# One channel scale and one channel bias per half step on VectorE, over two tiles at once, in the layer passes of a spectral image network

## The reference, cut to what matters

```
def layer_norm(x, g, b):
    mu = jnp.mean(x, axis=-1, keepdims=True)
    var = jnp.mean((x - mu) ** 2, axis=-1, keepdims=True)
    return (x - mu) * jax.lax.rsqrt(var + EPS) * g + b
...
for i in range(LAYERS):
    w1 = w1r[i] + 1j * w1i[i]
    w2 = w2r[i] + 1j * w2i[i]
    x1 = spectral_conv(h, w1, w2)
    x2 = jnp.einsum('bchw,oc->bohw', h, conv_w[i]) + conv_b[i][None, :, None, None]
    h = x1 + x2
    h = jnp.transpose(h, (0, 2, 3, 1))
    h = layer_norm(h, ln_g[i], ln_b[i])
    if i < LAYERS - 1:
        h = gelu(h)
    h = jnp.transpose(h, (0, 3, 1, 2))
```

## Time and profile before

| | |
|---|---|
| median of 3 runs | 3648.15 us (3635.49 to 3648.17) |
| profiled execution: its time, its span | 3639.14 us, 3637.3 us |
| PE busy | 3132.9 us, 86% |
| DVE busy | 2467.3 us, 68% |
| ACT busy | 2218.8 us, 61% |
| POOL busy | 2127.3 us, 58% |

### The profile page before, as it was taken

One profiled execution on the slowest core, in us unless ns is written; L12 is line 12 of the kernel. 1 busy time (PEld: TensorE's weight loads), 2 busy tenths in 40 slices (PEclk: granted clock), 3 DMA queues, 4 the chain that ended last, 5 costly groups with the idle time before them and its releaser, 6 DMA issues. The chain is left out here.

```text
span 3637.3 us, 202203 instructions
## 1 busy us (share of the span) xinstructions
PE 3132.9 (86%) x86496; PEld 2151.1 (59%) x86496; DVE 2467.3 (68%) x3756; ACT 2218.8 (61%) x3645; POOL 2127.3 (58%) x1147
## 2 busy tenths in 40 slices
PE   6777777999968999968999958999999986999998
PEld 3555556777756777756777753333333334666666
DVE  6665547888847888847888844444444436999996
ACT  4455445777745777746777736777777773555554
POOL 2322216888847888838888834444444434555554
PEclk8888887999988999979999978999999997999998
DMA  2232234555544556545555641211121111000000
GB/s 83 94 93 93 88 128 131 169 168 168 172 149 135 169 174 171 171 137 146 168 168 172 174 133 47 60 56 52 54 58 54 54 28 41 13 12 12 12 12 9
DMA packets 206411, 366.15 MB, mean 101 GB/s; under 512 B 107186, under 2 KB 124146, under 8 KB 206018
## 3 DMA queue, kind: packets, MB, share of 16 engines
q1 hardware_dynamic: 194610, 350.25, 32.5%
q10 hardware_dynamic: 7920, 10.03, 0.9%
q0 software_dynamic: 3744, 3.84, 0.7%
HBM read 206.31 MB, written 157.71 MB: 100 GB/s over the span
## 5 line engine op out<-in xcount | busy, mean ns | idle before, releaser
L1296 POOL TENSOR_TENSOR rstd<-var,mhalf 128x16 f32<-128x16 f32 x512 | 1537.4, 3018 | 773.9 <-DVE var L1073 767.2
L571 PE MATMUL ps<-d,hp 128*32 128x48 f32 x32768 | 492.9, 211 | 89.7 <-ACT asb L812 41.7
L571 PEld LDWEIGHTS ps<-d,hp 128*32 128x32 f32 x32768 | 410.2, 112 | 207.6 <-issue 106.3
L1073 DVE TENSOR_REDUCE var<-sq 128x16 f32<-128x528 f32 x384 | 402.8, 1050 | 146.3 <-ACT sq L772 146.2
L812 ACT COPY asb<-ps 128x384 f32<-128x384 f32 x512 | 254.3, 497 | 386.9 <-PE ps L571 264.8
L1087 DVE TENSOR_TENSOR zt<-ps,rstd 128x512 f32<-128x512 f32 x512 | 351.4, 686 | 200.0 <-POOL rstd L1296 195.5
L546 PE MATMUL ps<-ident,hp 128*128 128x128 f32 x2048 | 377.9, 309 | 12.7 <-ACT ho L796 10.0
L496 PEld LDWEIGHTS ps<-cwl,hc 64*64 64x64 f32 x16384 | 273.4, 139 | 146.9 <-issue 136.3
L772 ACT ACTIVATE sq<-ps 128x512 f32<-128x512 f32 x512 | 288.0, 599 | 115.4 <-PE ps L496 81.7
L507 PEld LDWEIGHTS ps<-dyi,gt 64*48 64x48 f32 x16384 | 234.7, 125 | 202.0 <-issue 190.0
L479 PE MATMUL ps<-zb,ex 48*128 48x512 f32 x1024 | 303.5, 668 | 53.8 <-issue 34.8
(11 more groups left out here) (171 smaller groups left out, 4881.3 us busy)
## 6 DMA issues: line engine op xcount, KB each, us to landing
h_scratch<-ho SPq DMA_DIRECT2D x256, 512.0 KB
hc<-h_scratch SPq DMA_DIRECT2D x256, 512.0 KB, 4.4
wsb<-in_w SPq DMA_DIRECT2D x64, 288.0 KB
gin<-g_scratch SPq DMA_DIRECT2D x252, 72.0 KB
gin<-g_scratch SPq DMA_DIRECT2D x504, 36.0 KB
g_scratch<-hp SPq DMA_DIRECT2D x32, 192.0 KB, 3.4
g_scratch<-hp ACTq DMA_DIRECT2D x32, 192.0 KB, 4.1
tokens<-wsb SPq DMA_DIRECT2D x256, 4.0 KB
```

What stands on the lines that cost most here:

```text
L571: last = nc.tensor.matmul(a_ps[row:row + 32, 2 * TRIG * k:2 * TRIG * k + 2 * TRIG], hp[b][:, u, 8 * j + k].rearrange("p v r -> p (v r)"), ...
L1073: nc.vector.tensor_reduce(dst, src, axis=AX.X, op=ALU.add).then_inc(var_ready, 1)
L1296: nc.gpsimd.tensor_tensor(rstd[u][:], var[u][:], mhalf[:], ALU.pow).then_inc(rstd_ready, 1)
```

## The change

`gain` and `bias` are no longer called once for each tile but once for each half step, over both tiles of `zt[h]` (128 x 1024 elements, with the 32 channel values spread over tiles and pixels by strides of zero). They stand behind the second `normalise`. A gelu of either tile waits for the one `bias` of its half step. The semaphores count accordingly.

```
-                act.wait_ge(zt_ready, 4 * (rank(s, g) - PAIRS) + 2 * h + u + 1)
+                act.wait_ge(zt_ready, 2 * (rank(s, g) - PAIRS) + h + 1)
...
-            def gain(s, g, h, u):
+            def gain(s, g, h):
 
-                z = zt[h][:, u].rearrange("p (c n) -> p c n", c=C)
-                dve.wait_ge(norm_ready, 4 * rank(s, g) + 2 * h + u + 1)
-                nc.vector.tensor_tensor(z, z, channels(s, 0).unsqueeze(2).to_broadcast([128, C, 16]), ALU.mult
+                z = zt[h][:].rearrange("p u (c n) -> p u c n", c=C)
+                dve.wait_ge(norm_ready, 4 * rank(s, g) + 2 * h + 2)
+                nc.vector.tensor_tensor(z, z, channels(s, 0).unsqueeze(1).unsqueeze(3).to_broadcast([128, 2, C, 16]), ALU.mult
                                         ).then_inc(gain_ready, 1)
...
                     here, old = where(i, p, 0, 0), where(i, p, 0, 1)
                     if old:
                         normalise(s, *old, 0)
-                        gain(s, *old, 0)
-                        bias(s, *old, 0)
                     if here:
                         reduce(s, *here, 0)
                     if old:
                         normalise(s, *old, 1)
-                        gain(s, *old, 1)
-                        bias(s, *old, 1)
+                        gain(s, *old)
+                        bias(s, *old)
                     if here:
                         reduce(s, *here, 1)
...
                     if here:
                         reduce(s, *here, 1)
                     if old:
-                        gain(s, *old, 1)
+                        gain(s, *old)
                     if nxt := where(i, p, 0, -2):
                         z_copy(s, nxt[0])
                     if old:
-                        bias(s, *old, 1)
+                        bias(s, *old)
```

More of the change, by code:

```diff
@@ L1115, in channels, with bias @@
                 return gbx[:, bass.ds(s, 1), which, :].rearrange("p a c -> p (a c)")
-            def gain(s, g, h, u):
-                z = zt[h][:, u].rearrange("p (c n) -> p c n", c=C)
-                dve.wait_ge(norm_ready, 4 * rank(s, g) + 2 * h + u + 1)
-                nc.vector.tensor_tensor(z, z, channels(s, 0).unsqueeze(2).to_broadcast([128, C, 16]), ALU.mult
+            def gain(s, g, h):
+                z = zt[h][:].rearrange("p u (c n) -> p u c n", c=C)
+                dve.wait_ge(norm_ready, 4 * rank(s, g) + 2 * h + 2)
+                nc.vector.tensor_tensor(z, z, channels(s, 0).unsqueeze(1).unsqueeze(3).to_broadcast([128, 2, C, 16]), ALU.mult
                                         ).then_inc(gain_ready, 1)
[L1124 to L1128, removed]
+            def bias(s, g, h):
+                z = zt[h][:].rearrange("p u (c n) -> p u c n", c=C)
+                dve.wait_ge(gain_ready, 2 * rank(s, g) + h + 1)
+                nc.vector.tensor_tensor(z, z, channels(s, 1).unsqueeze(1).unsqueeze(3).to_broadcast([128, 2, C, 16]), ALU.add
                                         ).then_inc(zt_ready, 1)
@@ L1269, in _ @@
             nc.vector.tensor_scalar(xsb[:, 0, :], xsb[:, 0, :], stem_gb[:, 3:4], None, ALU.add).then_inc(dc_ready, 1)
-            dve.sem_inc(gain_ready, 4 * PAIRS)
+            dve.sem_inc(gain_ready, 2 * PAIRS)
             dve.wait_ge(late_in, NLATE)
```

## The result

| | before | changed |
|---|---|---|
| median | 3647.64 us (3635.49 to 3648.17, 4 runs) | 4164.46 us (4158.39 to 4169.87, 4 runs) |
| profiled execution, its span | 3639.14, 3637.3 us | 4169.87, 4168.1 us |
| mean granted clock | 0.933 | 0.861 |

The changed kernel is slower: the ratio is 1.141, with a 95% interval of 1.1384 to 1.1436. The forecast was 4095 us, in a range of 3920 to 4250 us.

The account below looks back on a forecast made before the run. The prediction took a pass to be bound by PE. It summed 3639 us before, 288 for longer pairs, 5 for the last pairs and 158 for the clock to 4090, stated as 4095 us, range 3920 to 4250.

Parts of the forecast that it names:

- The operation over 1024 elements: On DVE, one merged gain or bias was taken at 1.22 us, like a plain add of 128 x 1024.
- The chain: Even half step, square through reduction, normalise, gain, bias, gelu and hc_copy to PE's turn: 6.12 us, before 2.73, turn 3.39 later.
- What is given back: After absorbed waits on ACT and PE, a pair gets 2.94 to 3.39 us longer, taken as 3.1; 93 pairs make 288 us.
- The clock's term: PE's clock falls behind the new idle gap: 5 us lower per pair at 0.34 us each, 1.7 us, 158 us in all.
- the 5 us of the last pairs: In each pass's last pair the gelu waits for four operations, not three short ones: 1.7 us, three times.
- The bound of 10 us: Rival: clock mostly at the lower level, 10 us in a pair, costing 3.5 us each; 4259 us, chance 0.1.
- The wait of L546 for L796: Sign in the later profile: PE waits for ACT's copy about 3.4 us once a pair, near 300 us in all.
- Costs taken at nothing: DVE's saving of 58 to 77 us counted as nothing; the odd half step's bias, half a us later, absorbed by ACT's idle 0.62.
- the two rules that disagreed: Skill guidance on DVE: group operations where saturated, saving an estimated 23 us; split them where unsaturated but making bubbles on others.
- chain, but the clock holds: Rival: the pairs lengthen but PE's clock does not fall; 3932 us, chance 0.2.
- Faster: Rival: DVE's queue decides a pair, so its 58 to 77 us less work give 3562 to 3581 us; chance 0.04.
- no change: Rival: the later gelu is hidden in ACT's 28% idle time; 3640 us, chance 0.05.

Follow-up runs that it names:

- fill_gap24: The changed kernel plus 24 unused transposes on PE ahead of the turn of (g-1,0), piece 1; ratio 1.084 to the kernel before, pair 17.95 us.
- act_order: The changed kernel with both gelus of (g-1,1) moved on ACT behind the two hc_copy, copy L826 and both coefficients; ratio 1.0163 to the kernel before, pair 15.43 us.
- place_only: The kernel before, its four operations of 512 kept but all placed behind the second normalise in the even half step; ratio 1.1037, pair 18.80 us.
- even_only: The kernel before with gain and bias merged only in the even half step; ratio 1.1427, pair 20.49 us.
- odd_only: The kernel before with gain and bias merged only in the odd half step; ratio 1.0031, pair 15.02 us.
- fill_gap: The changed kernel plus 14 unused transposes on PE ahead of the turn of (g-1,0), piece 1; ratio 1.0988 to the kernel before, pair 18.47 us.
- ahead: The changed kernel with the even half step's second normalise and merged gain and bias ahead of the first reduction; ratio 1.0559 to the kernel before, pair 17.06 us.

## Why the prediction was right

Point by point, by its own steps.

- **The operation over 1024 elements** was taken at 1.22 us; it measured 1.221 and 1.220.
- **The chain** of 6.12 us measured 6.07 us, the turn's delay of 3.39 us 3.34 (6.07 - 2.73).
- **What is given back**: 3.1 us a pair were taken between 2.94 and 3.39; fill_gap24, with the clock up, measured 3.07. Over 93 pairs it is 286 us; 288 were in the sum.
- **The cause**, ACT's queue behind the gelu and PE's queue behind the turn, is shown by act_order and place_only from two sides, and that it is the even half step alone by even_only and odd_only. Of the turn's delay place_only has 2.16 us from the new place and the other 1.18 us from the wait for both tiles; the sum had both, without telling them apart.
- **The clock's term was undersized.** The step "I take 5 us, nearer to the short case" and its price of 0.34 us gave 1.7 us for a pair. Measured: 6.8 us at the lower level in every pair, and 2.53 us of cost, or 0.37 us for each. That is 93 x 2.53 = 235 us in place of 158 us. The 77 us that are missing here account for the distance of 69 us between 4095 and 4164 us: with the measured terms the sum is 3639 + 286 + 5 + 235 = 4165 us, beside the profiled 4170. (No run shows the 5 us of the last pairs by themselves. The bound of 10 us was carried as 3.5 us a pair and 327 us in all; by the price of 0.34 it is 3.4 and 316.) The longer bound (10 us, 3.5 us) was the right side to lean to: PE's work behind the turn was dense, but 6.8 us of it passed before the clock was up.
- **The wait of L546 for L796** was forecast near 300 us with about 3.4 us once a pair; it is 316.6 us, with 3.28 us in the pair shown. ACT's L784 waits 3.28 us in the even half step, where some 3 us were forecast.
- **Costs taken at nothing**: DVE's saving of 58 to 77 us shows as 63 us of less busy time (2467.3 to 2404.3), and no run shows time won by it. The odd half step was taken at nothing; alone it costs 0.14 us a pair, and in the changed kernel nothing that can be told from none.

The rivals: "chain, but the clock holds" is what fill_gap24 made on purpose, at a ratio of 1.084; in the changed kernel it doesn't hold. "Faster" and "no change" needed DVE's queue to decide a pair or the gelu to have slack; in the trace after DVE waits 742.3 us for squares, 2.54 us of it at 889.24. Of the two rules that disagreed, the measurement went with the second: the Trainium skill (Perfetto Trace Analysis, Optimizing Scalar/DVE Operations) says that splitting instructions of an engine that isn't saturated but makes bubbles on others may let work finish sooner. This case's runs agree. The four short operations, with tile 0's ahead of the wait, are the split form, and it takes 12% less time. Most of that is the place, though: with all four behind the wait (place_only) a pair is 8% shorter than with the merged two (18.80 against 20.48 us).

## What to carry to other kernels

Before two operations are merged, look at what stands between them in the engine's order: if it is an instruction that waits for another engine, the merge ties the first half of the work to that wait. Then look at the queue of whoever uses the result: what is lost there is not the late operand's own delay but that of everything queued behind it, and the next engine's. And where a merge opens an idle gap on PE in each round, count the granted clock as a second term; here it was nearly as large as the first.

## What the runs showed of the hardware

- With idle gaps on PE of 2.1 us (place_only) and 3.3 us (changed) in each round of 18 to 20 us, the granted clock fell to 0.50 for 5.1 and 6.8 us of a pair in the mean; with 1.6 us (fill_gap) for 1.4 us; with 0.5 us (fill_gap24) and in act_order, with 0.6 us, never. The length of one gap does not tell it alone: early in the first pass of ahead the turn at 475.42 us had waited 0.79 us, the granted clock was 1.00 up to 474 us and 0.50 from 476 to 482 us. I had expected falls in most pairs; that they come in every pair of the changed kernel, and last 6.8 us though PE works without a gap from the turn on, I had not.
- A gain of DVE over 1024 elements took 2.00 us beside a tensor operation of POOL and 1.21 us alone, and POOL's own went from 0.67 to 1.41 us (ahead). A bias over 512 elements took 1.53 us in place of 0.69 (odd_only). The Trainium skill (SBUF — State Buffer, Who interferes with whom) says that a DVE instruction with two SBUF inputs contends with a GpSimd instruction that reads SBUF; these rows agree with it.
